# A graph kernel with a new order of work in each step, transposed one-hots made by TensorE, x's statistics in three parts, and twelve equal blocks

## The reference, cut to what matters

```python
# x (6144,128) float32, adj (6144,6144) int32, about 2 ones in a row
def _L0_gnn_ref(xx_anchor, input, adj, weight):
    anchor_adj = jnp.einsum('md,de,ne->mn', xx_anchor, weight, input)
    scores = jnp.where(adj > 0, anchor_adj, NEG_PAD)
    atten = jax.nn.softmax(scores / TEMPERATURE, axis=1)
    return atten @ input
def _L1_gnn_ref(input, W, a, adj, M):
    h = input @ W
    e = jax.nn.leaky_relu((h @ a_src)[:, None] + (h @ a_dst)[None, :], negative_slope=ALPHA)
    valid = (adj > 0) & (h.sum(axis=1) != 0)[None, :]
    att = jnp.where(valid, jax.nn.softmax(jnp.where(valid, e, NEG), axis=1), 0.0)
    L = valid.sum(axis=1).astype(h.dtype)
    top = att.max(axis=1)
    attention = jnp.where((top > THR)[:, None], jnp.where(att >= THR, att, 0.0) * L[:, None], 0.0)
    return jax.nn.elu(h + attention @ h)
h = jnp.maximum(_layernorm(x, axis=-1), 0.0)
x = x + _L0_gnn_ref(h, L0_gnn_input, adj, L0_gnn_weight)
h = jnp.maximum(_layernorm(x, axis=-1), 0.0)
return x + _L1_gnn_ref(h, L1_gnn_W, L1_gnn_a, adj, 6144)
```

## Time and profile before

| | us |
|---|---|
| median of 3 runs (lowest, highest) | 859.21 (854.74, 864.99) |
| the profiled execution: its time | 865.55 |
| its span, first to last instruction | 863.8 |
| VectorE busy | 535.6 (62%) |
| TensorE busy | 411.7 (48%) |
| ScalarE busy | 389.3 (45%) |
| GpSimd busy | 328.8 (38%) |
| HBM read and written | 179.73 MB, 6.37 MB |

### The profile page before, as it was taken

One profiled execution on the slowest core, in us unless ns is written; L12 is line 12 of the kernel. 1 busy time (PEld: TensorE's weight loads), 2 busy tenths in 40 slices (PEclk: granted clock), 3 DMA queues, 4 the chain that ended last, 5 costly groups with the idle time before them and its releaser, 6 DMA issues. The chain is left out here.

```text
span 863.8 us, 9189 instructions
## 1 busy us (share of the span) xinstructions
PE 411.7 (48%) x2773; PEld 270.6 (31%) x2806; DVE 535.6 (62%) x2015; ACT 389.3 (45%) x395; POOL 328.8 (38%) x358
## 2 busy tenths in 40 slices
PE   2355564646573737476674755543000420107474
PEld 0012323333342424243433343333000420007474
DVE  0077576959696969696877779793310431128995
ACT  4388485756575857576675843421000110001222
POOL 5002324150606060606446462757777037720000
PEclk9678777879788988878777777756555555557877
...
GB/s 332 423 420 395 311 321 272 335 249 347 235 380 231 371 262 350 283 330 293 285 330 259 346 256 180 120 42 51 47 56 53 7 69 53 54 25 40 72 75 88
DMA packets 38037, 186.75 MB, mean 216 GB/s; under 512 B 7904, under 2 KB 9184, under 8 KB 19424
## 3 DMA queue, kind: packets, MB, share of 16 engines
...
...
HBM read 179.73 MB, written 6.37 MB: 215 GB/s over the span
## 5 line engine op out<-in xcount | busy, mean ns | idle before, releaser
L854 ACT ACTIVATE arena<-arena,half_c 128x2048 bf16<-128x2048 int32 x144 | 282.9, 1996 | 54.6 <-DMA arena<-in_adj 52.5
L788 POOL DMA_INDIRECT X<-in_L_gnn_input,idx_all x138 | 142.5, 1033 | 353.7 <-DVE idx_near L1095 315.3
L1431 PE MATMUL K<-arena,bits 128*128 128x512 bf16 x546 | 182.4, 464 | 151.7 <-ACT arena L854 130.7
L1431 PEld LDWEIGHTS K<-arena,bits 128*128 128x128 bf16 x576 | 59.0, 112 | 235.3 <-ACT arena L854 148.5
L809 POOL DMA_INDIRECT arena<-table,idx_near x96 | 91.9, 957 | 62.3 <-DMA table<-hs 33.4
L1020 DVE MAX8 keys<-K 128x8 int32<-128x128 f32 x192 | 42.5, 283 | 72.1 <-PE K L1431 71.6
L809 POOL DMA_INDIRECT E<-table,idx_near x48 | 49.6, 1034 | 14.5 <-issue 13.1
L1442 PE MATMUL G<-g,R_all 128*128 128x128 bf16 x333 | 34.3, 279 | 33.8 <-DVE g L1142 22.7
L1442 PEld LDWEIGHTS G<-g,R_all 128*128 128x128 fp8e4 x333 | 31.5, 131 | 41.0 <-DVE g L1142 22.8
L1485 PE MATMUL SB<-pick,RT_all 128*128 128x48 bf16 x144 | 6.4, 192 | 78.1 <-DVE pick L1133 78.1
L1125 DVE TENSOR_TENSOR G<-G,X 128x384 f32<-128x384 f32 x35 | 19.6, 561 | 36.8 <-remote 24.0
...
## 6 DMA issues: line engine op xcount, KB each, us to landing
...
x_all<-in_x SPq DMA_DIRECT2D x1, 2816.0 KB, 17.9
...
arena<-table,idx_near POOLq DMA_INDIRECT x96
```

The source lines that it names most:

```text
L788: pool.indirect_dma_start(out=x_of(b)[:, e, :], out_offset=None, in_=inp, in_offset=bass.IndirectOffsetOnAxis(ap=idx_all[:, at:at + 1], ax ...
L854: nc.scalar.activation(sign[:, load % RING, :], ring[:, load % RING, :], ACT.Sign, bias=half_c[:], scale=1.0).then_inc(signed, 1)
L1431: last = mm(bank_[:], bits[:, third * TB + j, :], sign[:, load % RING, j * FOLD:(j + 1) * FOLD], start=False, stop=(third == G - 1 and j = ...
```

## The change

There are five parts.

1. Twelve equal blocks of four tiles. The program by hand for the last blocks is gone; the loops run over n from 0 to NB + 4, and a part is called when its block exists.
2. `RT_all` is made by TensorE and ScalarE: `make_RT` multiplies the transposed steps of `below` with `step_of` (12 matmuls of 128x128 in three groups into banks G1, G0, G1), and `keep_RT` copies each group as fp8. VectorE's comparison at L1098 is gone, the width of a list's record goes from 34 to 33, and with it two constants that GpSimd made.
3. The statistics of x come from `norms_of_x(k)`, which handles 16 tiles at once, in the steps 0, 1 and 2, behind the last find and ahead of `inp_sum` (L1257). `norms` handles the hidden rows of b3 alone.
4. The order of the parts within a step is new on ScalarE, VectorE and TensorE. `exponent` moves to the head of the next step, `edge_shares` too, `project_hx` and `project_hid` come after it, `keep_high` and `keep_h` after four converts instead of one, and `differences` at the end of VectorE's step.
5. On GpSimd the last block's `neighbours` comes before its `mean`, and with one block less the early `records(0, i)` are four calls instead of five.

The diff, cut to its core:

```diff
-    SIZES = [B] * (T // B - 1) + [B // 2] * 2
+    SIZES = [B] * (T // B)
+    PART = 16
...
-    LW = 2 * SLOTS + 2
+    LW = 2 * SLOTS + 1
...
                 mean(NB - 2)
+                neighbours(NB - 1)
                 mean(NB - 1)
-                neighbours(NB - 1)
...
+                def keep_RT(b):
+
+                    for i in range(0, SIZES[b] * G, 4):
+                        width = min(4, SIZES[b] * G - i)
+                        act.wait_ge(RT_made, RPARTS[b] + i // 4 + 1)
+                        nc.scalar.copy(RT_all[:, bass.ds(FROM[b] * G + i, width), :],
+                                       one_hot_bank(parts_of(b) + i // 4)[:, 0:width * P].rearrange("p (e r) -> p e r", r=P),
+                                       saturate=False).then_inc(RT_r, 1)
...
+                    if 0 <= b3 < NB:
+                        exponent(b3)
                     more(1)
-                    if b2 >= 0:
+                    if 0 <= b4 < NB:
+                        hidden(b4)
+                    more(2)
+                    if 0 <= b3 < NB:
+                        exponent_of_edges(b3)
+                    if 0 <= b4 < NB:
+                        keep_turned(b4)
+                    more(1)
+                    if 0 <= b1 < NB:
+                        hidden_x(b1)
+                    if 0 <= b4 < NB:
+                        keep_h(b4)
+                    if 0 <= b2 < NB:
                         keep_high(b2)
...
-                    tt(RT_all[:, edges(b), :], iota1_b[:].unsqueeze(1).broadcast_to([P, n_e, P]),
-                       led[:, 0:n_e, LW - 1:LW].broadcast_to([P, n_e, P]), ALU.is_equal, saturate=False).then_inc(RT_r, 1)
...
+                def make_RT(b):
+
+                    n = parts_of(b)
+                    for k in range(n):
+                        width = min(4, SIZES[b] * G - 4 * k)
+                        if n + k - 2 < n:
+                            pe.wait_ge(R_r, RPARTS[b] + n + k - 1)
+                        else:
+                            pe.wait_ge(RT_r, RPARTS[b] + k - 1)
+                        for e in range(4 * k, 4 * k + width):
+                            last = mm(one_hot_bank(n + k)[:, (e - 4 * k) * P:(e - 4 * k + 1) * P], below[:, e, :], step_of[:],
+                                      start=True, stop=True)
+                        last.then_inc(RT_made, 1)
```

366 lines of the change are left out of this document (143 added, 223 removed).

## The result

The changed kernel takes 864.47 us (median of 20 runs, 859.24 to 866.16), the kernel before 860.22 us (20 runs, 853.10 to 866.24): a ratio of 1.0052, 95% interval 1.003 to 1.0073. Beside later experiments it was 0.9999 (0.9964 to 1.0033) and 1.0057 (1.0027 to 1.0086). I had forecast 0.98. The profiled execution took 866.14 us, its span is 864.2.

What follows compares the result with a forecast made beforehand. Waits, not any engine, were taken to set the 44.75 us step; 33.6 + 1.6 + 1.0 + 3.8 made 40.0. With 8 lost in the start, records at 686 plus 159.7 gave 846, 841 on the median; range 808 to 874.

Steps and rivals of the forecast that it cites:

- 7.3 in each of steps 0, 1 and 2: VectorE in the start: norms_of_x handles 16 tiles at once, 7.3 us per step; the start loses 8 by decode(2).
- counted out: VectorE's waits before L1140 (2.91) and L1106 (2.56) taken as gone, since the new order moves keep_high and keep_h.
- VectorE's sum: VectorE's work per step: 34.56 less 2.98 for RT_all and four moments of x, 31.6 us; 33.6 with gaps.
- (a): Chain to columns_of_edges: make_R waits for spread_used, then keep_R and the lists; 1.6 us a step.
- (b): record now comes before spread_lists and may wait for keep_h; 1.0 us a step.
- (c): The step's end: edge_shares and the last folds fall into the gather burst; 3.8 us, bounds 0 and 9.7.
- TensorE's sum: TensorE's work per step: 24.08 plus about 1 us for 12 short matmuls, 25.1, hidden under VectorE's 33.6.
- The tail: From decode(11) at 514: gathers and a mean 132.5, table wait 39, third block of records at 686 against 704.08.
- C: Rival, 0.18: the burst replaces the removed waits, holding edge_shares or last folds to its end; step 45.9, 881 us.
- C's milder case: Half of the steps held to the burst's end: a step of 44.5 and 869 us.
- D: Rival, 0.15: steps as forecast, but a whole last block lies open in the tail; 851 us, up to 859.
- B: Rival, 0.22: counts come promptly, the step's end costs 0 to 1; steps of 37 and 39, 810 us.

Runs made afterwards that it cites:

- norms_quiet: Changed kernel with parts 1 and 2 of x's statistics moved ahead of columns_of_edges in steps 1 and 2: 0.9896 of the kernel before, 859.9 us.
- RT_vector: Changed kernel with RT_all made on VectorE again by one comparison, without make_RT and keep_RT: 1.0082 of the kernel before.
- blocks13: Changed kernel with thirteen blocks, eleven of four tiles and two of two, in the uniform loops: 0.9892 of the kernel before.
- hid_first_again: Changed kernel with turn_hid ahead of edge_shares and project_hx: 1.0156 of the kernel before with late counts; 0.9898 in the earlier set (hid_first), where none were late.

## Why the prediction was wrong

The direction failed, by two terms. One is the start's, "7.3 in each of steps 0, 1 and 2". The other is the step's waits: I had "counted out" 2.91 and 2.56 and let only the step's end pay for late counts, with nothing for `turn_hid`'s, which holds ScalarE for 6.43. I give the terms in order.

- **The start**: decode(0) at 72.84, forecast 73. Step 1 took 37.67, not 30.5; step 2 took 45.52, not 37.5. The term "7.3 in each of steps 0, 1 and 2" was priced outside a burst and placed in one: 3.94 and 4.03 of waits for own counts and operations of 1.2 and 1.6. decode(2) is 15.0 later than forecast. norms_quiet shows it: 16.6 come back at decode(2), about 10 of them for good.
- **VectorE's sum**, 31.6 a step: 33.39. L1098's 1.75 went, and `decode`, which now meets `mean`, got slower by 1.7. By RT_vector the removal is worth about 0.6 a block in the time, and nothing that its trace shows.
- **The waits**: (a) 2.55, not 1.6; (b) 0, not 1.0, but 1.44 before L1070; (c) "the step's end, 3.8": 2.42 and 1.4 in `decode`. So of the 3.2 that this step is too long, 1.8 are work and 1.4 are waits (7.8, not 6.4). The sum of the waits is close, and still the reasoning was wrong. I had "counted out" 2.91 and 2.56 with the sentence that what `project_hx` and `project_hid` feed "is read a few converts later". I didn't look at `turn_hid`, which the order puts behind `edge_shares` and `project_hx`, in the burst: its count is held for 6.4, ScalarE's converts and TensorE's next groups stand behind it, and the chain to the next indices begins there. Before, that chain began at the copy of `hs`, at 277.63, by `mean`'s end at 277.66, and the next burst 26.9 later. The change shortened the chain by about one us and the burst by 0.7, and left the circle: 43.0 a step against the 40.0 forecast. TensorE's sum failed with it: 29.6 a step, not 25.1. `make_RT` itself takes the 1.0 forecast (0.61 and 0.40); much of the rest goes with the granted clock of 0.78 instead of 0.89, which falls behind that wait.
- **Steps 3 to 7** took 41.7 on average, forecast 40: step 3, behind the late start, took only 36.0. **Steps 8 to 11**: 44.4 (42.3, then three of 45.1), forecast 43.25. decode(11) at 542.43, 28 later than forecast.
- **The tail**: 162.4 from decode(11) to the third block of records, forecast 172; the last indices 50.0 behind decode(11), forecast 55, the table's wait 34.05, forecast 39. This is 9.6 better than forecast, and still twelve equal blocks are the worse choice: blocks13 is 9.4 us faster.

15.0 + 13.4 (nine steps) − 9.6 − 0.3 is 18.5, the distance from the 845.7 forecast for the span to 864.2.

Of the rivals, C named the mechanism, that the burst takes the place of the waits removed, and its arithmetic of the step, 27.6 + 17.9 + 0.4 = 45.9, is nearly what hid_first_again measured (45.0), where `edge_shares` is held to the burst's end. In the changed kernel `edge_shares` came 2.7 late only. C's milder case doesn't come out as written: half of the steps at 45.9 and half at the forecast's mean of 41.4 make 43.7, not 44.5. By the Trainium skill (TensorE: Matmul & The Clock Gate, "Architectural detail: the array is 16× 32×32, not 1× 128×128") the 64 entries of TensorE's queue would have been the reason. The trace speaks against it: in the tail `rows`, 12 matmuls behind 13.54 of idle time, had its count 20 us late, though TensorE had executed nothing just before them. What delays the counts no run here shows. D, that the tail gives the gain back, isn't what came: its condition, steps as forecast, failed, and the tail was better than forecast. That a whole last block is dear (9.4) is what it had right. B's steps of 37 to 39 exist, where gathers are few (38.45) or counts not late (39.6 with hid_first).

My range, 808 to 874, held the time; the 0.64 for faster by over 1% was the error. I saw that TensorE's counts were late in bursts, and priced the new order by VectorE's busy time plus waits. Where one late count sits in a loop that leads back to the burst, the step is to be priced by going round that loop.
